# Feed-forward sums on GpSimd, normalisation on ScalarE: one fused transformer layer on Trainium2

## The reference

```python
def _L0_ffn_ref(x, W_fc, ln_w, ln_b, W_proj):
    h = jnp.einsum('btd,hd->bth', x, absmean(W_fc))     # 256 -> 1024, weights rounded to -1, 0, 1
    h = jax.nn.gelu(h, approximate=False)
    h = layernorm(h, ln_w, ln_b)                        # over the 1024 inner channels
    return jnp.einsum('bth,dh->btd', h, absmean(W_proj))

x = L0_attn_x
xn = _layernorm(x, axis=-1)
x = x + _L0_attn_ref(xn, ...) + _L0_ffn_ref(xn, ...)    # 16 heads of 16, causal, rotary
```

## Time and profile before

| quantity | value |
|---|---|
| median of 3 runs | 1882.07 us (1881.39 to 1882.36) |
| the profiled execution's own time | 1882.02 us |
| span of its trace, first to last instruction | 1880.3 us |
| second stage, from the first GELU to the last `R` | 43.0 to 492.1 us |
| TensorE busy, whole span | 1818.9 us (97%) |
| VectorE busy | 1671.0 us (89%) |
| ScalarE busy | 1590.6 us (85%) |
| GpSimd busy | 535.9 us (28%) |

### The profile page before, as it was taken

How to read it: one execution, slowest core, us unless ns; L and a number is a source line. 1 busy time by engine, 2 the same in 40 slices (tenths; PEclk the granted TensorE clock), 3 DMA queues, 4 the chain that set the end, 5 groups by cost and what they waited for, 6 DMA issues and landing times.

```text
span 1880.3 us, 41858 instructions
## 1 busy us (share of the span) xinstructions
PE 1818.9 (97%) x13875; PEld 682.6 (36%) x13875; DVE 1671.0 (89%) x4759; ACT 1590.6 (85%) x1924; POOL 535.9 (28%) x647
## 2 busy tenths in 40 slices
PE   5999999999799999999999999999999999999998
PEld 3555555655322323223232322323232322323223
DVE  5899999999899999999999999999999999999962
ACT  4675676676169999999999999999999999999994
POOL 1121121121343141433414142341415234141220
PEclk9999999999779999999999999999999999999999
DMA  5233333235531304042331415133141413314112
GB/s 191 63 105 89 88 102 97 84 101 120 107 74 32 65 17 65 22 73 33 70 63 40 65 45 92 32 75 59 44 65 45 86 37 76 59 44 65 36 49 67
DMA packets 160324, 129.01 MB, mean 69 GB/s; under 512 B 95344, under 2 KB 144752, under 8 KB 159768
## 3 DMA queue, kind: packets, MB, share of 16 engines
q1 hardware_dynamic: 158776, 126.45, 30.9%
q10 hardware_dynamic: 1376, 0.43, 0.1%
HBM read 74.60 MB, written 42.98 MB: 63 GB/s over the span
## 4 chain that ended last, share of the span: by engine, by line
PE 42%; ACT 15%; issue 8%; DVE 5%; DMA 1%; POOL 1%; SPq 1%; ACTq 0%; DVEq 0%; POOLq 0%
PE pv L1754 16%; ACT prob L1532 13%; PE sm L1716 10%; PE st L1739 10%; PE sm L1687 3%; PE st L1726 2%; DVE sm L1615 2%; ACT excess L1525 1%; DVE sm L1603 1%; PE sm L1680 1%; DVE pm L1620 1%; DMA scratch_i<-inverse 1%; DVE pm L1603 1%; DVE pm L1615 1%; ACT Y L1515 0%
## 5 line engine op out<-in xcount | busy, mean ns | idle before, releaser
L1532 ACT ACTIVATE prob<-st 128x1024 f32<-128x1024 f32 x1088 | 1048.3, 1028 | 53.8 <-PE st L1739 43.5
L1754 PE MATMUL pv<-prob,V 128*32 128x512 f32 (+3 forms) x5120 | 586.4, 539 | 0.3 <-ACT Y L1515 0.2
L1603 DVE CUSTOM_DVE_ANT_0 sm<-sm,mask 128x256 f32<-128x256 f32 (+3 forms) x1024 | 473.8, 521 | 32.4 <-PE sm L1716 27.8
L1716 PE MATMUL sm<-K,Q 48*128 48x512 f16 (+3 forms) x2112 | 480.1, 349 | 13.3 <-DVE pm L1603 5.6
L1739 PE MATMUL st<-Q,K 50*128 50x512 f16 (+3 forms) x2560 | 479.2, 352 | 10.2 <-ACT prob L1532 6.2
L1620 DVE TENSOR_REDUCE pm<-sm 128x1 f32<-128x512 f32 x640 | 412.4, 684 | 35.1 <-PE sm L1716 31.7
L1491 POOL TENSOR_SCALAR_AFFINE_SELECT prob<-prob 128x256 f32<-128x256 f32 (+1 forms) x448 | 190.6, 439 | 867.7 <-ACT prob L1532 863.1
L1615 DVE CUSTOM_DVE_ANT_0 sm<-sm,excess 128x512 f32<-128x512 f32 x448 | 301.3, 712 | 18.1 <-PE sm L1716 17.2
L1716 PEld LDWEIGHTS sm<-K,Q 48*128 48x128 f16 x2112 | 152.3, 95 | 328.0 <-DVE pm L1615 114.1
L1739 PEld LDWEIGHTS st<-Q,K 50*128 50x128 f16 x2560 | 126.2, 94 | 363.0 <-ACT prob L1532 265.6
L1525 ACT ACTIVATE excess<-st 128x1024 f32<-128x1024 f32 x218 | 220.5, 1025 | 9.1 <-DVE pm L1620 5.1
(11 more groups left out here) (201 smaller groups left out, 1900.3 us busy)
## 6 DMA issues: line engine op xcount, KB each, us to landing
Q<-scratch_q SPq DMA_DIRECT2D x102, 128.0 KB, 4.3
K<-scratch_k SPq DMA_DIRECT2D x102, 128.0 KB, 7.1
x<-in_x SPq DMA_DIRECT2D x16, 512.0 KB, 4.5
scratch_v<-Rt SPq DMA_DIRECT2D x64, 128.0 KB, 2.0
scratch_r<-Rt SPq DMA_DIRECT2D x16, 512.0 KB, 3.2
V_raw<-scratch_v SPq DMA_DIRECT2D x16, 512.0 KB, 9.5
Yc<-Y SPq DMA_DIRECT2D x124, 64.0 KB
spread<-scratch_i SPq DMA_DIRECT2D x124, 64.0 KB, 2.2
```

The costliest lines, as they stand in the source:

```text
L1532: act.activation(prob_of(quad, k)[:, :, :], st[number % ST][:, :, :], ACT.Exp).then_inc(exp_done, 1)
L1603: i = dve.tensor_tensor_reduce(x, x, mask[:, CH - block_width(t, k):], 1.0, -3e38, ALU.add, ALU.max, best(h, t, k))
L1716: i = pe.matmul(dst[:, at:at + width], lhsT=Q[slot][r, h // 2, t * P:(t + 1) * P], rhs=K[slot][r, h // 2, k * CH:k * CH + width], start=Tr ...
L1754: i = pe.matmul(pv[2 * DH * h:2 * DH * (h + 1), CH - width:CH], lhsT=V[quad % VSLOTS][:, j, h, :], rhs=prob_of(quad, u)[:, h % 2, at:at + ...
```

## The change

Three things are changed in the second stage.

1. A new tile `gsum` [128, 2, 512] takes the sum of inner blocks 0 to 4, of the values and of the squares at once. GpSimd makes it with four instructions in a chunk (`add_inner`), each 128x1024 in fp32. The first two stand ahead of `rstd` in GpSimd's order, the other two behind it and ahead of `xc`. Each waits for the square of its block, and from the second on for the sum before it. TensorE's `sum_strips` then has four inputs (`gsum` and the blocks 5, 6 and 7), so 8 products in place of 16, and waits for all four additions.
2. `sum_strips` moves on TensorE from ahead of `down_projection(ch, 0)` to behind it.
3. The four instructions that write `xn` leave VectorE and go to ScalarE (`normalise`), behind the values and ahead of the copy of the strips. VectorE keeps `nmr` and releases ScalarE through `nmr_ready`. ScalarE's loop now holds two chunks in a turn.

```diff
--- before.py
+++ after.py
@@ -559,6 +559,7 @@
         gh = sb("gh", [P, HC, CH], fp16)
         gl = sb("gl", [P, HC, CH], fp16)
         strips = sb("strips", [P, CH])
+        gsum = sb("gsum", [P, 2, CH])
         fst = sb("fst", [P, SUB, 2])
         fmm = sb("fmm", [P, SUB])
         fve = sb("fve", [P, SUB])
@@ -588,6 +589,8 @@
         h_read = sem("h_read")
         gh_ready = sem("gh_ready")
         g2_ready = sem("g2_ready")
+        gsum_steps = sem("gsum_steps")
+        nmr_ready = sem("nmr_ready")
         gl_ready = sem("gl_ready")
         strips_summed = sem("strips_summed")
         strips_ready = sem("strips_ready")
@@ -607,6 +610,7 @@
 
         qk_v = [scr[m].rearrange("a b (h e) t -> a b h e t", e=DH) for m in ("Q", "K")]
         STORES = 2 * 3 * PARTS
+        ADDS = 4
 
         @block.sync
         def _(sp):
@@ -664,12 +668,24 @@
                 pool.tensor_tensor(out=xc[par][:, :, :], in0=X[par][:, :, :],
                                    in1=w["CB"][:, None, :].to_broadcast([P, SUB, C]), op=ALU.add).then_inc(xc_ready, 1)
 
+            def add_inner(ch, n):
+
+                pool.wait_ge(g2_ready, ch * HC + n + 2)
+                if n:
+                    pool.wait_ge(gsum_steps, ch * ADDS + n)
+                first = gsum[:, :, :] if n else g[:, 0, :, :]
+                pool.tensor_tensor(out=gsum[:, :, :], in0=first, in1=g[:, n + 1, :, :], op=ALU.add).then_inc(gsum_steps, 1)
+
             add_constant(0, 16)
             def body(i2, par, last):
                 ch = i2 * 2 + par
+                for n in range(2):
+                    add_inner(ch, n)
                 if not last:
                     pool.wait_ge(stats_ready, ch + 2)
                     rsqrt(rstd, ve).then_inc(rstd_ready, 1)
+                for n in range(2, ADDS):
+                    add_inner(ch, n)
                 pool.wait_ge(R_ready, ch + 1)
                 if not last:
                     add_constant(1 - par, i2 * 16 + 16 + 16 * par)
@@ -684,7 +700,7 @@
 
         @block.vector
         def _(dve):
-            me = Steps(dve, steps, 13)
+            me = Steps(dve, steps, 12)
             spare = dve.alloc_register("spare_of_dve")
 
             def stats(x, loaded, count):
@@ -699,15 +715,10 @@
                 me.wait()
                 dve.tensor_scalar(ve[:, :], mv[:, :, 1], LN_EPS, None, ALU.add).then_inc(stats_ready, 1)
 
-            def normalise(x, count):
+            def shift(count):
                 dve.wait_ge(rstd_ready, count)
-                me.done(dve.scalar_tensor_tensor(out=nmr[:, :], in0=mv[:, :, 0], scalar=-1.0, in1=rstd[:, :],
-                                                 op0=ALU.mult, op1=ALU.mult))
-                me.wait()
-                for s in range(SUB):
-                    i = dve.tensor_scalar(xn[:, s, :], x[:, s, :], rstd[:, s:s + 1], nmr[:, s:s + 1],
-                                          ALU.mult, ALU.add)
-                i.then_inc(xn_ready, 1)
+                dve.scalar_tensor_tensor(out=nmr[:, :], in0=mv[:, :, 0], scalar=-1.0, in1=rstd[:, :],
+                                         op0=ALU.mult, op1=ALU.mult).then_inc(nmr_ready, 1)
 
             def low_x(turn):
 
@@ -764,7 +775,7 @@
                     low_g(ch, hc)
                 if not last:
                     dve.wait_ge(xT_in_psum, ch * 2 + 2)
-                    normalise(X[1 - par], ch + 2)
+                    shift(ch + 2)
                 low_g(ch, 5)
                 read_plain(0, ch)
                 low_g(ch, 6)
@@ -820,11 +831,18 @@
                 act.wait_ge(qk_ready, ch * 4 + 2 * m + 1)
                 act.activation(part[2 * m][:, 0, :], bank[2 * m][:, :], ACT.Copy, scale=w["qscale"][:, 0:1]).then_inc(high_ready, 1)
 
+            def normalise(ch, x):
+
+                act.wait_ge(nmr_ready, ch + 1)
+                for s in range(SUB):
+                    i = act.activation(xn[:, s, :], x[:, s, :], ACT.Identity, bias=nmr[:, s:s + 1], scale=rstd[:, s:s + 1])
+                i.then_inc(xn_ready, 1)
+
             def strips_evac(ch):
                 act.wait_ge(strips_summed, ch + 1)
                 act.activation(strips[:, :], strip_bank[:, :], ACT.Copy).then_inc(strips_ready, 1)
 
-            def body(ch, last):
+            def body(ch, par, last):
                 for hc in range(HC + 1):
                     if hc < HC:
                         act.wait_ge(h_ready, ch * HC + hc + 1)
@@ -842,13 +860,17 @@
                     act.wait_ge(v_ready, ch * 2 + k + 1)
                     act.activation(Vs[:, 2 * k:2 * k + 2, :], hidden_bank[k][:, :].rearrange("p (s c) -> p s c", s=2),
                                    ACT.Copy, scale=w["pall"][:, 2:3]).then_inc(v_read, 1)
+                if not last:
+                    normalise(ch, X[1 - par])
                 strips_evac(ch)
                 if not last:
                     xT_evac(ch + 1)
 
-            with act.Fori(0, NCH - 1) as ch:
-                body(ch, False)
-            body(NCH - 1, True)
+            with act.Fori(0, NCH // 2 - 1) as i2:
+                for par in range(2):
+                    body(i2 * 2 + par, par, False)
+            for par in range(2):
+                body(NCH - 2 + par, par, par == 1)
 
         @block.tensor
         def _(pe):
@@ -869,11 +891,13 @@
             def sum_strips(ch):
 
                 pe.wait_ge(g2_ready, ch * HC + HC)
+                pe.wait_ge(gsum_steps, ch * ADDS + ADDS)
+                inner = [gsum[:, :, :]] + [g[:, hc, :, :] for hc in range(ADDS + 1, HC)]
                 for k in range(2):
-                    for hc in range(HC):
-                        q = hc % 4
-                        i = pe.matmul(strip_bank[STRIP * q:STRIP * (q + 1), :], lhsT=w["strip"][:, k, :, :].rearrange("p a k -> p (a k)"),
-                                      rhs=g[:, hc, k, :], start=hc + 4 * k < 4, stop=hc + 4 * k >= 8, tile_position=(0, STRIP * q))
+                    for q, x in enumerate(inner):
+                        i = pe.matmul(strip_bank[STRIP * q:STRIP * (q + 1), :],
+                                      lhsT=w["strip"][:, k, :, :].rearrange("p a k -> p (a k)"), rhs=x[:, k, :],
+                                      start=k == 0, stop=k == 1, tile_position=(0, STRIP * q))
                 i.then_inc(strips_summed, 1)
 
             def query_keys(ch, t, cc):
@@ -916,9 +940,9 @@
                                 i = pe.matmul(hidden_bank[k][:, a * C:(a + 1) * C], lhsT=x[:, cc, s * P:(s + 1) * P],
                                               rhs=w[half][:, cc, :], start=cc + n == 0, stop=cc + n == CC + 1)
                     i.then_inc(v_ready, 1)
-                sum_strips(ch)
                 pe.wait_ge(gl_ready, ch * HC + HC)
                 down_projection(ch, 0)
+                sum_strips(ch)
                 down_projection(ch, 1)
                 pe.wait_ge(v_read, ch * 2 + 2)
                 pe.wait_ge(strips_ready, ch + 1)
```

## The result

| | before | after |
|---|---|---|
| median of 4 runs | 1882.09 us | 2008.80 us (2006.09 to 2012.95) |
| ratio, 95% interval | | 1.0673 [1.066, 1.0687] |
| profiled execution, span | 1882.02, 1880.3 us | 2012.95, 2011.2 us |
| first GELU to last `R` | 449.1 us | 579.7 us |
| mean chunk | 27.86 us | 36.29 us |

The change makes the kernel 6.7% slower. The second stage took 130.6 us more in the profiled executions (579.7 against 449.1), which is all of the difference: what lies ahead of it grew by 2.2 us, what lies behind it shrank by 2.

A forecast was written before the change was run, and what follows sets the result against it. TensorE sets the pace, busy 27.62 of 27.80 us. Stalls and strips 7.0 plus clock 1.65 make 8.6 us a chunk; 14 chunks 120, first about 6, last about 4: 130 on 1882.02 gives 2012 us, range 1955 to 2038.

The forecast's parts named there:

- While GpSimd adds, VectorE's instructions with two SBUF inputs stand still: In the second stage, each GpSimd addition holds such a VectorE instruction for 2.1 us; the others go on.
- The rival that only `xc` causes the stalls: Stalls belong to `xc` alone, so the four new additions are free: 1868 us, or 1853 with `xc` free too; chance 6%.
- the rival that half of them vanish: Two of four additions fall beside VectorE instructions they do not hold: 1945 us, chance 10%.
- Which stalls there would be: VectorE in a chunk: stalls of 2.1, 2.1, 1.5 and 2.1 us, less 1.3 for the normalisation: 6.5 us.
- the walk: Step through VectorE's order in one chunk, placing each addition and `xc`: last `gl` from 16.6 to 23.1 us.
- The last `gl` at 23.1: VectorE's last `gl` ends 23.1 us after the chunk's first GELU, in place of 16.6; TensorE's down-projection then starts at 23.2.
- The clock, 1.65 us a chunk: After 8.7 us idle, TensorE restarts the down-projection at 1.2 GHz; 3.3 us at half speed cost 1.65 us a chunk.
- The clock stays up: Rival: VectorE's stalls are there, but TensorE keeps its full clock through the wait: 1986 us, chance 18%.
- The step beyond the rows, that one SBUF input can be free as well: VectorE instructions with one SBUF input outside two-port modes do not meet GpSimd; the rows showed it for PSUM operands only.
- Normalisation on ScalarE at no cost: ScalarE's four `xn` instructions take 1.5 us, between 0 and 2.4, within some 9 us of idle time; costed at nothing.
- First chunk about +6, last about +4: First chunk has one stall less, about 6 us longer; in the last, waiting absorbs part, about 4 us.
- What the change would bring if additions were free: Down-projection waits for the last `gl` at 15.3; a chunk gains 0.9 us, by 16 = 14 us, 1868 us.

The follow-up runs named there:

- gl_psum: The changed kernel with the second operand of `gl` read from a PSUM bank instead of from `gh` in SBUF: 1866.5 us, ratio 0.9916.
- write_only: The changed kernel with each of GpSimd's four additions replaced by three fills behind a one-column addition: 1874.8 us, ratio 0.9957.
- adds_unused: The kernel before with GpSimd's four additions put in at their new places and their sums unused: 2015.2 us, ratio 1.0707.
- clock_fill: The changed kernel with 32 useless TensorE products a chunk between the values and the first down-projection: 1979.4 us, ratio 1.0515.
- adds_free: The changed kernel without GpSimd's four additions, `gsum` filled once: 1858.7 us, ratio 0.9873.
- new_order_all16: The changed kernel without the additions, with all 16 products at the strips' new place and normalisation on ScalarE: 1885.1 us, ratio 1.0009.
- xn_only: The kernel before with only the normalisation moved to ScalarE and ScalarE's loop of two chunks: 1881.0 us, ratio 0.9987.
- timed_two: The changed kernel with two additions, 12 products, waits placing GpSimd's additions and `xc`, and strips behind the third down-projection group: 1872.8 us, ratio 0.9949.
- two_untimed: The two-addition, 12-product version of the changed kernel with later strips, without the three added waits on GpSimd: 1969.4 us, ratio 1.0458.

## Why the prediction was right

The forecast was 2012 us, the median is 2008.8 and the profiled execution 2012.95. Point by point:

- *While GpSimd adds, VectorE's instructions with two SBUF inputs stand still*: shown, by gl_psum (the operand moved, the loss gone) and write_only (GpSimd as busy, but not reading, the loss gone). The rival that only `xc` causes the stalls fell with adds_unused, and the rival that half of them vanish with the trace: 63 of the 128 `gl` and all 15 `nmr` are long, five in a middle chunk: each addition and `xc` held one, the fourth addition for 1.4 us and the others for about 2.1.
- *Which stalls there would be*: 2.1 + 2.1 + 1.5 + 2.1 in the walk; 5.62 - 1.41 = 4.2, then 4.92 - 1.41 = 3.5 measured. Right.
- *The last `gl` at 23.1*: 22.4. The walk took over VectorE's start in the chunk from before. There VectorE was behind: TensorE began the means at 208.48 and VectorE read the first at 209.32, 0.84 us later. In the kernel after it waits for them and reads 0.32 us behind their start (295.94), and its `R` ends 0.5 us earlier, at t = 4.5. The chunk at full clock came out at 34.1 (clock_fill), where 34.8 stood. `R` ends at t = 4.5 in adds_free, new_order_all16 and xn_only too, where VectorE is relieved of `xn`, so the first two beat their expectations.
- *The clock, 1.65 us a chunk*: 36.29 - 34.09 = 2.2 us in the profiled executions, of which that of the kernel after was the slowest of its four; by the medians 29.4 us in all, 1.9 a chunk. The term was too small, because half speed lasted 3.0, 5.0 or 6.0 us; the row of before had one case, 3.3. Against the 34.19 us of a middle chunk in clock_fill these cases cost 1.5, 2.4 and 2.9 us, half of their length, as the prediction reckoned.
- What the Trainium skill says (TensorE: Matmul & The Clock Gate, "What's actually happening"), that the point of the switch varies with where the work lands, gave the right warning. The Trainium skill puts that variation at ±500 ns; here the slow part varied by 3 us, and the measurement decides.
- *Luck*: the two errors, -0.7 and +0.55 a chunk, nearly cancel, so the closeness of the total is partly luck.
- *The clock stays up*, the rival at 1986 us: it fell, with 0.50 granted behind each long wait and 29 us gained by clock_fill.
- *The step beyond the rows, that one SBUF input can be free as well*: the Trainium skill (SBUF — State Buffer, "Who interferes with whom") says so of instructions outside the two-port modes. The statistics agree (0.41 us each beside an addition in gl_psum). `ve` (a `tensor_scalar`) would be the exception, if it is in such a mode. That it is was not tested.
- *Normalisation on ScalarE at no cost*: right. It took 2.07 us there (1.5 was taken, 2.4 the bound) and ended at 280.20, 11 us ahead of the transposes at 291.25.
- *First chunk about +6, last about +4*: 33.76 against 28.28 is +5.5, and 35.4 against 31.2 from first GELU to last `R` is +4.2.
- *What the change would bring if additions were free*: 14 us forecast, 24 measured. The 0.6 us by which the last `gl` came earlier than 15.3 makes 10 of them.
- Two of the rivals' times are off by 2 us in their own sums: half the stalls gives 1947 (2012 less 15.5 by 4.2), and `xc` free as well 1855 (TensorE cannot start ahead of t = 14.5). No chance hangs on either.

## What to carry to other kernels

Look for instructions whose duration is far above their usual one while nothing releases them; here one `nmr` of 2.35 us in place of 0.15 told the price of every addition that was going to be given to the other engine. Idle time of GpSimd is not free time: an instruction there that reads SBUF belongs beside VectorE instructions that read PSUM, and the waits that delay it on purpose were worth 97 us here. Count spare time only on the side of the wait that matters, and add to every TensorE wait of several microseconds what the slower clock costs behind it (1.5 to 2.9 us here).

## What the runs showed of the hardware

- A VectorE `tensor_scalar` of 128x4 with one SBUF input (`ve`) is held by a GpSimd addition (0.70 us in timed_two and 1.54 in gl_psum in place of 0.17), while `bn_stats` with one SBUF input is not (0.41).
- GpSimd fills that only write held no VectorE instruction with two SBUF inputs (0.75 us for a `gl` on median), except such as were started behind a held `ve`; `ve` itself took 0.83 to 1.73 us beside one fill or two (write_only).
- TensorE went to half speed within a wait of 4.45 us in each middle chunk of two_untimed. Behind waits of 7.9 us in the kernel after it stayed there for 3.0, 5.0 or 6.0 us of work.
- Products of 32 columns in fp32 cost by rounds of four, 0.9 us a round of 512 tokens: 3.57, 2.7 and 1.86 us for 16, 12 (or 10) and 8.
